# Attention scores: six bf16 products in contractions of 96 become fp32 contractions of 16, four heads in four row tiles

## The reference

```
q, k, v = x_normed @ Wq.T, x_normed @ Wk.T, x_normed @ Wv.T     # heads of 16 channels
score = einsum('bhnd,bhmd->bhnm', q, k) * 0.25                  # 128 heads (8 batches x 16)
attn  = softmax(where(causal, score, -inf)); out = attn @ v
x = x + layernorm(out @ Wo.T)
x = x + layernorm(two experts of 8 for each token, weighted by a softmax over the top two)
```

## Time and profile before

| | us |
|---|---|
| time, median of 3 runs (2004.69 to 2005.61) | 2004.83 |
| the profiled execution | 2003.3 |
| its span on the core | 2001.5 |
| PE busy | 1863.6 |
| DVE busy | 1589.5 |
| ACT busy | 1324.0 |
| POOL busy | 934.5 |
| first exponential of the attention starts | 95.3 |
| last exponential of the attention starts | 1178.0 |

### The profile page before, as it was taken

The page is one execution under the profiler, slowest core; times in us unless marked ns, Lnnn a source line. Parts: engine busy times, 40 slices in busy tenths (PEclk is TensorE's granted clock), DMA queues, the critical chain, the costliest instruction groups (busy, mean ns, idle before and its releaser), DMA issues.

```text
span 2001.5 us, 76386 instructions
## 1 busy us (share of the span) xinstructions
PE 1863.6 (93%) x26830; PEld 1283.6 (64%) x26831; DVE 1589.5 (79%) x5285; ACT 1324.0 (66%) x3387; POOL 934.5 (47%) x1439
## 2 busy tenths in 40 slices
PE   6799999999999999999999899999999999999980
PEld 3244555455555455455444359899999999999980
DVE  3888888888888888888888748778777777777767
ACT  5277788878888888888777775554444444544436
POOL 4333344456656566565555654554323333333335
PEclk9799999999999999999999999999999999999995
DMA  6734656475555646464547378889889989898848
GB/s 204 212 119 128 192 170 207 150 217 167 184 168 162 191 146 201 139 190 154 169 145 232 109 231 259 238 248 261 257 258 261 263 259 263 261 267 243 244 121 338
DMA packets 257628, 411.79 MB, mean 206 GB/s; under 512 B 36912, under 2 KB 194352, under 8 KB 250160
## 3 DMA queue, kind: packets, MB, share of 16 engines
q1 hardware_dynamic: 217856, 363.46, 56.3%
q0 software_dynamic: 29680, 35.41, 9.5%
q10 hardware_dynamic: 9792, 8.93, 1.5%
HBM read 284.83 MB, written 122.28 MB: 203 GB/s over the span
## 4 chain that ended last, share of the span: by engine, by line
PE 81%; DVE 9%; issue 4%; ACT 3%; DMA 2%; SPq 1%; POOL 0%; DVEq 0%; ACTq 0%; POOLq 0%
PE ps_s L1540 18%; PE ps_o L1424 11%; PE ps_s L1372 10%; PE ps_w L1372 10%; PE ps_e L1372 10%; PE ps_e L1540 6%; PE ps_e L1557 6%; PE ps_o L1557 6%; DVE cmax L797 3%; DVE arena L794 2%; PE ps_e L1550 1%; DVE space L128 1%; ACT arena L1164 1%; PE ps_w L1500 1%; PE ps_w L1437 1%
## 5 line engine op out<-in xcount | busy, mean ns | idle before, releaser
L1164 ACT ACTIVATE arena<-ps_e 128x512 f32<-128x512 f32 (+3 forms) x1536 | 686.4, 496 | 211.2 <-PE ps_e L1372 204.0
L1372 PE MATMUL ps_s<-arena 96*32 96x512 bf16 (+3 forms) x6144 | 506.6, 334 | 31.8 <-DVE mrow L804 12.5
L1372 PE MATMUL ps_e<-arena 98*32 98x512 bf16 (+3 forms) x6144 | 517.8, 330 | 10.6 <-ACT arena L1164 8.3
L797 DVE TENSOR_REDUCE cmax<-ps_s 128x1 f32<-128x512 f32 x512 | 338.0, 680 | 21.7 <-PE ps_s L1372 20.4
L1372 PEld LDWEIGHTS ps_s<-arena 96*32 96x32 bf16 x6144 | 173.9, 96 | 219.5 <-DVE rmax L794 101.1
L794 DVE CUSTOM_DVE_ANT_0 arena<-ps_s,c,cmax 128x128 bf16<-128x128 f32 (+3 forms) x512 | 268.1, 541 | 51.3 <-PE ps_s L1372 46.1
L1424 PE MATMUL ps_o<-arena 128*32 128x512 f32 (+3 forms) x3072 | 296.4, 487 | 3.4 <-ACT ot L1178 2.8
L794 DVE CUSTOM_DVE_ANT_0 arena<-ps_s,c 128x128 bf16<-128x128 f32 (+3 forms) x512 | 234.0, 491 | 61.7 <-PE ps_s L1372 58.7
L669 POOL DMA_INDIRECT acc<-blank,place_now x135 | 213.1, 1578 | 142.0 <-DMA acc<-blank,place_now 63.9
L1372 PEld LDWEIGHTS ps_e<-arena 98*32 98x32 bf16 x6144 | 175.3, 97 | 155.8 <-issue 54.9
L686 POOL TENSOR_SCALAR_AFFINE_SELECT arena<-arena 128x512 f32<-128x512 f32 x256 | 162.6, 635 | 241.1 <-ACT arena L1164 240.4
(11 more groups left out here) (182 smaller groups left out, 2983.8 us busy)
## 6 DMA issues: line engine op xcount, KB each, us to landing
arena<-in_gate_up SPq DMA_DIRECT2D x91, 1024.0 KB, 5.9
arena<-qk_parts SPq DMA_DIRECT2D x384, 128.0 KB, 3.0
c_h<-in_gate_up SPq DMA_DIRECT2D x44, 1024.0 KB
qk_parts<-space SPq DMA_DIRECT2D x120, 192.0 KB
d_xin<-xs SPq DMA_DIRECT2D x136, 130.5 KB, 3.2
arena<-v_aug SPq DMA_DIRECT2D x32, 512.0 KB, 6.0
o_t<-ot SPq DMA_DIRECT2D x64, 256.0 KB, 2.6
v_aug<-space SPq DMA_DIRECT2D x28, 512.0 KB, 5.3
```

The source lines that it names most:

```text
L797: dve.reduce_max(cmax[:, par, i - NB:i - NB + 1], ps_s[:, m % RS, 0:w], AX.X).then_inc(s_cmax, 1)
L1164: act.activation(pw[:, at % RP, begin:end], ps_e[:, n % RE, 0:w], ACT.Exp, scale=SCALE).then_inc(e_done, 1)
L1372: last = pe.matmul(out[at:at + QUAD], lhsT[:, at:at + QUAD], rhs, start=start, stop=stop)
```

## The change

Scores are contracted in fp32 over the 16 channels themselves. The four heads of a quad lie side by side in the partitions: head `s` of the quad has rows `32 s` to `32 s + 15` of `qs` and `ks`, and row `32 s + 16` of `qs` holds its maximum, that of `ks` minus one. A score matmul of head `s` therefore stands on a tile of 32 rows and 32 columns of the array. The order in a slot is now exp, max, exp, max, ..., with the maxima of heads 2, 3, 0, 1 beside the exponentials of heads 0, 1, 2, 3 (`BESIDE_EXP`), and the blocks of the maxima are put in an order in which they are as wide as the exponentials of the same slot (`MAXC`). All four heads' maxima of a quad are finished together: one small maximum on DVE (`both_halves`), one matmul with the identity into `ps_w` on PE (`max_rows`), one copy on ACT, one transfer. The splitting into parts is gone, and so is the store of three parts: one store of fp32 for each pair of token tiles, and eight loads of 16 rows for each quad where there were twelve of 16 rows for four heads. Other work in a slot, which stood behind the first, second and third `s`, now stands behind the second alone.

```
-ROWS = 6 * DH
-ROWS_M = ROWS + 2
+ROWS_M = DH + 1
...
-    SETS, AHEAD = 3, 6
-    MAXC = [(i, 0, (i + 1) * P) for i in range(NB)]
-    MAXC += [(i, k0, min(HALF, (i + 1) * P - k0)) for i, k0 in ((4, 0), (5, 0), (4, HALF), (6, 0), (5, HALF), (7, 0), (6, HALF), (7, HALF))]
+    SETS, AHEAD = 3, 18
+    BEGIN = -AHEAD
+    BLOCKS = [(i, k0, min(HALF, (i + 1) * P - k0)) for i in range(SB) for k0 in range(0, (i + 1) * P, HALF)]
+    MAXC = []
+    for c in range(NM):
+        MAXC.append(next(block for block in BLOCKS if block[2] == EXPC[(c + BEGIN + 1) % NE][2] and block not in MAXC))
+    BESIDE_EXP = (2, 3, 0, 1)
...
-                for z, often in ((0, 3), (1, 2), (2, 1)):
-                    for k in range(often):
-                        rows = slice(nth, ROWS, ROWS // DH)
-                        sp.dma_start(qs[rows, u * 4:u * 4 + 4].rearrange("r h t -> r (h t)"),
-                                     qk_v[b, 0, s // 2, s % 2, z]).then_inc(loads[u], 16)
...
+                for r in range(4):
+                    rows = slice(r * QUAD, r * QUAD + DH)
+                    sp.dma_start(qs[rows, u], qk_v[b, 0, s // 2, s % 2, r]).then_inc(loads[u], 16)
+                    sp.dma_start(ks[rows, u], qk_v[b, 1, s // 2, s % 2, r]).then_inc(loads[u], 16)
...
+            def both_halves(n):
+
+                dve.wait_ge(s_cmax, (n + 1) * NM * 4)
+                dve.tensor_tensor(rmax[:, n % 2, :, NB:SB], rmax[:, n % 2, :, NB:SB], cmax[:, n % 2], ALU.max).then_inc(s_rmax, 1)
...
-                by_columns(ps_s[:, m % RS, 0:w], qs[0:ROWS, slot, i * P:(i + 1) * P], ks[0:ROWS, slot, k0:k0 + w],
+                by_columns(ps_s[:, m % RS, 0:w], qs[r:r + DH, u, i * P:(i + 1) * P], ks[r:r + DH, u, k0:k0 + w],
                            start=True, stop=True).then_inc(s_scores, 1)
...
-                by_columns(ps_e[:, n % RE, 0:w], ks[0:ROWS_M, slot, j * P:(j + 1) * P], qs[0:ROWS_M, slot, q0:q0 + w],
+                by_columns(ps_e[:, n % RE, 0:w], ks[r:r + ROWS_M, u, j * P:(j + 1) * P], qs[r:r + ROWS_M, u, q0:q0 + w],
                            start=True, stop=True).then_inc(e_scores, 1)
...
                 for s in range(4):
                     m = (g - BEGIN) * 4 + s
+                    if 0 <= g + 1 < NE * QUADS:
+                        exp_scores(g + 1, s)
                     if 0 <= m < HEADS * NM:
                         max_scores(m)
-                    if NM <= m < HEADS * NM + NM and m % NM == ROWS_AT:
-                        max_rows(m // NM - 1)
-                    if 0 <= g + 1 < NE * QUADS:
-                        exp_scores(g + 1, s)
-                    if s == 0:
+                    if s == 1:
```

More of the change, by code:

```diff
@@ L349, in attention_layer @@
         first_x = [ps_s[:, 2, u * D:u * D + D].rearrange("p (k t) -> p k t", k=KT) for u in range(2)]
-        rows_tile = ps_s[0:2 * SB, RS - 1, 0:P // 2].bitcast(BF16)
         loads, v_loads = ([sem(f"{n}{s}") for s in range(SETS)] for n in ("loads", "v_loads"))
         rows_in, ones, carried = sem("rows_in"), sem("b_ones"), sem("b_carried")
-        s_scores, s_cmax, s_mhi, s_mlo = (sem("s_" + n) for n in ("scores", "cmax", "mhi", "mlo"))
+        s_scores, s_cmax, s_rmax = (sem("s_" + n) for n in ("scores", "cmax", "rmax"))
         rows_ps, rows_sb = sem("rows_ps"), sem("rows_sb")
@@ L418, in vout_of, with qk_of @@
             return arena[:, at:at + 1024].rearrange("p (s c h d) -> p s c h d", s=4, c=2, h=4)
[L420 removed]
+        def qk_of(a):
             if 2 <= a < EARLY:
[L422 to L424 removed]
+                return pw[:, 2 * (a - 2):2 * (a - 1)].rearrange("p a b -> p (a b)").rearrange("p (m t) -> p m t", m=4)
+            return qk_sb[:, a % 2]
         def w_view(bank):
@@ L735, in _ @@
                     pool.tensor_tensor(x1_sb[:, u], y[:, u], cx[:, u], ALU.add).then_inc(c_x1, 1)
-                for a in due(A_AT, 6, g):
-                    third(a, 1)
-                for a in due(A_AT, 3, g):
-                    third(a, 0)
                 for i in due(S_AT, 0, g):
@@ L1088, in _ @@
                             place(n, 0)
-                        for a in due(A_AT, 2, g):
-                            remainder(a, 0)
-                        for a in due(A_AT, 4, g):
-                            remainder(a, 1)
                         for a in pairs_due(-5, -15, g):
@@ L1375, in max_scores @@
             def max_scores(m):
-                head, c = divmod(m, NM)
-                i, k0, w = MAXC[c]
-                slot = head % (SETS * 4)
-                if c == 0 and head % 4 == 0:
-                    pe.wait_ge(loads[head // 4 % SETS], (head // (SETS * 4) + 1) * LOADS * 16)
+                n, at = divmod(m, NM * 4)
+                i, k0, w = MAXC[at // 4]
+                r, u = BESIDE_EXP[at % 4] * QUAD, n % SETS
+                if at == 0:
+                    pe.wait_ge(loads[u], (n // SETS + 1) * LOADS * 16)
@@ L1392, in max_rows @@
-                pe.wait_ge(s_cmax, min((n + 1) * NM + ROWS_AT + 2 - RS, HEADS * NM))
-                pe.transpose(rows_tile, mpart[:].rearrange("p z i -> p (z i)"), ident_b).then_inc(rows_ps, 1)
+                bank_free()
+                used.append((rows_sb, n + 1))
+                pe.wait_ge(s_rmax, n + 1)
+                pe.matmul(ps_w[0:4 * SB, 0:P], rmax[:, n % 2].rearrange("p r i -> p (r i)"), consts["ident"],
+                          start=True, stop=True).then_inc(rows_ps, 1)
             def exp_scores(g, s):
```

173 lines of the change are left out of this document (60 added, 113 removed).

## The result

The changed kernel takes 2656.0 us (median of 5 runs, 2632.0 to 2724.3) against 2004.83, which is 651 us more; the prediction had 256 more and a range up to 2600. The ratio of the two kernels is 1.321 (interval 1.318 to 1.324), from its three runs that weren't slowed further by a lower clock; the profiled execution is the slowest of the five (2724.3 us), some 2.6% above the median. In the experiments the kernel before took 2024 to 2034 us, so their totals are compared by ratio.

What follows compares the result with a forecast made beforehand. PE was taken as the bound, needing 32.4 of 34.65 us a quad. Terms of -0.3 + 4.4 + 3.6 + 2.1 - 0.3 - 1.5 gave +8.0 us a quad, +256 us over 32 quads: 2261 us, range 2080 to 2600.

Steps and rivals of the forecast that it cites:

- PE's clock is full: Starting step: PE's clock is full from the third slice almost to the end, so all is counted at 2.4 GHz.
- changes of tile: PE switching between 32x32 tiles and tiles of all rows: 36 more switches a quad at 0.10 us, +3.6 us.
- other waits: PE's waits in a quad, some 2.2 us, of which the lighter DVE and ACT and equal widths give back 1.5.
- Passes against tiles: PE's score streaming: fp32 on four row tiles at once takes 15.5 us a quad against bf16's 15.8, -0.3 us.
- the rival with two or none at a time: Score row tiles don't all overlap on PE: 2597 us with two at a time, 3538 with none; chances 0.04 and 0.03.
- Issue: Fourth group of a run on PE starts 0.21 us late, delaying the block behind: 21 runs a quad, +4.4 us.
- Three banks: Score groups waiting for their bank in three runs of eight groups: 0.7 us each, +2.1 us a quad.
- What goes: Work removed a quad: 0.3 us on PE, 3.1 on DVE, about 2 on ACT; the latter two pay only in PE's waits.
- the balance of widths: Maxima as wide as the exponentials beside them; shares in the 1.5 us a quad given back from PE's waits.
- the block on all rows: Sign in PE's order: it should start 0.1 us after the last score group's streaming ends; sooner means free tile changes.
- both other engines were under 75%: Sign: ACT and DVE both under 75% busy; DVE near 95% would mean PE is not the bound.
- the distance of sixteen copies: Sign in the changed profile: the copies of finished outputs over sixteen quads should stand 680 us apart.

Runs made afterwards that it cites:

- e2_rows32: The changed kernel with score contractions over all 32 rows of a tile, the added rows adding nothing: 1.1753 of the kernel before.
- micro_b: Not the kernel: only rounds of four row tiles, 16 and 32 rows in turn, paced by VectorE with small gaps; clock low at 16 rows, full at 32.
- micro_a: Not the kernel: matmuls alone in dense stretches without readers, row tiles of 16 or 32 rows and bf16 groups; a 512-wide round took 1.02 us with either.
- e1_late_rows: The changed kernel with PE's step on the maxima's rows at the end of its slot and the halves joined before the next maximum: 1.3212 of the kernel before.
- e6_before_again: The kernel before, unchanged, traced again on a chip of the experiments: 35.2 us for a steady quad.
- e5_bf16_quads: Half of the change: four heads' maxima together at the exponentials' width, score products left in bf16 as before: 0.9924 of the kernel before.
- e4_late_rows32: The changed kernel with both edits, 32-row score contractions and the later step on the maxima's rows: 1.1703 of the kernel before, 45.8 us a quad.
- micro_c: Not the kernel: dense rounds of four 32-row tiles at four widths: 1.02, 0.94, 0.91, 0.91 us a round at 512, 384, 256, 128 columns.

## Why the prediction was wrong

**The step that failed** is the first one: "PE's clock is full [...] so what follows is counted at 2.4 GHz". That row tells the clock of the work before. The change took 80 of 96 and 81 of 98 rows out of the scores' contractions, and PE's clock went with them: 1.00 to 0.78 in the quads. `e2_rows32` gives the price, by filling up the rows with zeros: 0.146 of before, 293 us of the 651. `micro_b` shows the cause without the kernel: 16 rows with small gaps fall to the lower level, 32 rows with the same gaps don't, and by `micro_a` 16 rows without gaps don't either. At four row tiles it takes both. Which of the kernel's gaps matter wasn't separated: taking one away, the stall of 1.0 us, left the clock at 0.83 in `e1_late_rows`.

**The sum at full clock** was mis-sized, 8.0 us a quad against 10.9 (46.1 less the 35.2 of `e6_before_again`). The step that failed here is the banks and the waits: the prediction let them grow by 0.6 us a quad (2.1 for the banks, less 1.5 of waits given back). Its terms, beside the sixteen quads of `e2_rows32`, read run by run as above:

| term, us a quad | predicted | measured |
|---|---|---|
| streaming of the scores | 15.5 | 15.3 |
| issue and changes of tile (4.4 + 3.6; 20 runs of 0.24 + 0.15) | 8.0 | 7.8 |
| three banks: runs of two rounds | 2.1 | 4.4 |
| other waits (2.2 - 1.5) | 0.7 | 2.3 |
| all other work of PE (32.4 - 15.8 - 0.3) | 16.3 | 16.3 |
| sum | 42.6 | 46.1 |

- *Passes against tiles* was right: four row tiles run at once, and the rival with two or none at a time is out.
- *Issue* and *changes of tile* were right in their sum. How the 0.39 of a run divides between them, no run shows. Groups start 0.03 us apart and not 0.07, because only the first four of a group's eight records stand ahead of the next group. The Trainium skill, page "TensorEngine Tiling (Array Packing)", Key Properties, says that a change of tiling mode drains TensorE. The prediction's estimate by that rule comes to 4.4 + 36 x 0.2 = 11.6 us, which the measured 7.8 doesn't bear out. Its estimate by the 10.6 times that the Trainium skill's page "TensorE: Matmul & The Clock Gate", Measured speedup vs the span model, gives for sixteen tiles was 23.4 us for streaming and issue, without the changes; the trace has 23.1 with them. In the dense rounds of 512 columns sixteen tiles gave 16 x 0.85 / 1.02 = 13.3 times.
- *Three banks* was right in place, the rounds with nothing between them, and half of the size: four runs of two rounds that wait 1.1 us on average, for three of 0.7.
- *What goes*: DVE and ACT got lighter (63% and 60% in the quads of `e2_rows32`), though by 1.7 and 0.7 us a quad and not by 3.1 and 2; neither was the bound. But PE's waits did not shrink; even with the balance of widths alone (`e5_bf16_quads`) the steady quads were no faster. The new step for four heads' maxima brought two waits of its own. One is the 1.0 us for the joined maxima, whose removal gave 0.3 (`e4_late_rows32`). The other stands before the router's product, which waits until ACT has copied the maxima's rows out of `ps_w`. In `e2_rows32`:

```profile
723.03 0.44 PE L1313 MATMUL ps_w<-w_r,h_t 128*32 128x8 f32 x32 [0.94 <-ACT mrow L1122]
```

The measured base is part of the difference too: a quad of before took 0.5 us more in `e6_before_again` (35.2) than in the prediction's trace (34.65).

Of the expected signs, the block on all rows stood about where it was forecast and both other engines were under 75%; the distance of sixteen copies was 883 us and not 680.

**The account of the 651 us**: 0.146 x 2005 = 293 for the clock, 0.175 x 2005 = 351 at full clock, of which 256 were predicted; the other 95 are what the banks and the waits cost above their terms. Together that is 644, or 0.321 of before; the 651 at the top is the difference of the medians of all runs.

## What to carry to other kernels

A full PE clock in a profile belongs to the work that is there. When a change takes rows out of PE's contractions and leaves gaps between them, count it at the lower level too; filling a contraction up to all rows of its tile cost no time in PE (a round took 1.02 us with 16 rows and with 32), and here gave back 0.146 of the time of before. Row tiles that run together also hold their banks together: put a block of other work between two rounds, or count a bank's wait for each run of rounds. Read a price for the kernel in the kernel's own trace: a mean over a long dense stretch can hold pauses that the kernel doesn't have. And where a change has two halves, try each alone: the half that was not about PE was the one worth having (0.992).

## What was not expected of the hardware

- The granted clock fell with the rows at work: 0.50 at 16 rows and 1.00 at 32, both paced alike, in eight stretches out of eight; 1.00 at 16 rows without gaps, and 0.50 for a single row tile of 16 rows without gaps.
- Even 32 rows didn't always hold it: in the stretch of 128 columns in `micro_c`, with its pauses, the clock fell, while at 256 columns, with pauses alike, it stayed at 1.00.

```profile
270.00:318.00 48.00, 33.75 (x1594) 25.83 (x1602) 0.00 (x0) 0.00 (x0) 0.54 0.01 4
```

- There it cost nothing: with its pauses the stretch of 128 columns took 0.91 us a round at half the clock, as that of 256 did at the full one.
- In the dense stretches of 256 and 128 columns PE paused about 1 us after every four rounds, without a wait that the profile shows, and so took 28 ns for each of its records on average (0.91 us for 32), though within a group records start 7 ns apart (four in 0.03 us).
